# Joining two of three attention exponentials per group into one 1,024-column ScalarE instruction in a fused macaron transformer block

## The reference

```python
x = x + 0.5 * ffn(layernorm(x), W_up, W_gate, W_down)    # ternary weights, silu(up) * gate
x = x + attn(layernorm(x), Wq, bq, Wk, bk, Wv, bv)
x = x + 0.5 * ffn(layernorm(x), W_up, W_gate, W_down)
# attn: 16 query heads of 16 features, 4 key/value groups (4 query heads each), causal
scores = einsum('bhqd,bhkd->bhqk', q, k) / sqrt(d);  scores above the diagonal = -inf
out = einsum('bhqk,bhkd->bhqd', softmax(scores), v)
```

## Time and profile before

| | |
|---|---|
| median of three executions | 584.15 us |
| the profiled execution | 583.65 us |
| its span, first to last instruction | 581.9 us |
| TensorE busy | 554.8 us, 95% |
| VectorE busy | 480.2 us, 83% |
| ScalarE busy | 399.2 us, 69% |
| GpSimd busy | 168.5 us, 29% |
| 192 score matmuls (L1339) | first 206.9 us, last 409.2 us |
| 192 exponentials (L598), busy | 123.7 us |

### The profile page before, as it was taken

The page is one execution under the profiler, slowest core; times in us unless marked ns, Lnnn a source line. Parts: engine busy times, 40 slices in busy tenths (PEclk is TensorE's granted clock), DMA queues, the critical chain, the costliest instruction groups (busy, mean ns, idle before and its releaser), DMA issues.

```text
span 581.9 us, 12392 instructions
## 1 busy us (share of the span) xinstructions
PE 554.8 (95%) x4244; PEld 343.9 (59%) x4244; DVE 480.2 (83%) x1862; ACT 399.2 (69%) x716; POOL 168.5 (29%) x264
## 2 busy tenths in 40 slices
PE   2989999999999989999999999998999999999998
PEld 2445556656566756666566666554455656656566
DVE  6898978998875889999999998996897688666664
ACT  5857655765745469798888888887665765765642
POOL 3115201101440033555556463666301101110100
PEclk9999999999999999999999999999999999999999
DMA  8711101100104161323323323221302211111112
GB/s 304 235 30 37 19 19 37 37 20 19 38 0 116 34 148 58 90 73 85 102 52 103 85 67 85 69 50 39 38 1 58 52 55 55 37 56 55 36 37 73
DMA packets 72222, 37.90 MB, mean 65 GB/s; under 512 B 35520, under 2 KB 71616, under 8 KB 72128
## 3 DMA queue, kind: packets, MB, share of 16 engines
q1 hardware_dynamic: 72160, 37.11, 24.7%
HBM read 18.22 MB, written 10.49 MB: 49 GB/s over the span
## 4 chain that ended last, share of the span: by engine, by line
PE 77%; DVE 15%; ACT 3%; issue 2%; POOL 2%; DMA 1%; DVEq 0%; ACTq 0%; POOLq 0%
PE bank L1178 33%; PE bank L1190 17%; DVE sm_out L994 6%; PE bank L1339 5%; PE bank L1282 5%; PE bank L1309 5%; PE bank L1350 5%; PE bank L1364 2%; PE bank L1355 2%; PE bank L1154 1%; DVE hid L858 1%; DVE stats L738 1%; POOL xn L415 1%; ACT shared L598 1%; DVE hl L873 1%
## 5 line engine op out<-in xcount | busy, mean ns | idle before, releaser
L488 ACT ACTIVATE silu<-bank,w_scale 128x512 f32<-128x512 f32 x128 | 87.3, 683 | 114.1 <-PE bank L1178 114.1
L994 DVE CUSTOM_DVE_ANT_0 sm_out<-bank,mask 128x256 f16<-128x256 f32 (+1 forms) x512 | 151.0, 351 | 12.3 <-PE bank L1309 11.6
L858 DVE SCALAR_TENSOR_TENSOR hid<-silu,h_unit,bank 128x512 f32<-128x512 f32 x128 | 95.0, 743 | 63.5 <-ACT silu L488 63.1
L1190 PE MATMUL bank<-wT_down,hh 128*128 128x256 f16 x512 | 118.3, 273 | 2.5 <-DVE hl L873 2.3
L1190 PE MATMUL bank<-wT_down,hl 128*128 128x256 f16 x512 | 118.2, 272 | 0.0
L1178 PE MATMUL bank<-xh,wT_up 128*128 128x512 f16 x256 | 98.0, 383 | 1.1 <-DVE xl L802 0.7
L873 DVE TENSOR_TENSOR hl<-hid,hh 128x512 f16<-128x512 f32 x128 | 98.8, 772 | 0.0
L1178 PE MATMUL bank<-xh,wT_gate 128*128 128x512 f16 x256 | 97.3, 380 | 1.0 <-DVE hid L858 1.0
L1178 PE MATMUL bank<-xl,wT_up 128*128 128x512 f16 x256 | 98.0, 383 | 0.0
L1178 PE MATMUL bank<-xl,wT_gate 128*128 128x512 f16 x256 | 97.3, 380 | 0.0
L424 POOL TENSOR_TENSOR xnl<-xn,xnh 128x1024 f16<-128x1024 f32 x13 | 28.3, 2176 | 211.0 <-ACT xn L527 177.8
(11 more groups left out here) (134 smaller groups left out, 795.1 us busy)
## 6 DMA issues: line engine op xcount, KB each, us to landing
q_st<-q_scratch SPq DMA_DIRECT2D x32, 256.0 KB
q_scratch<-q_hl SPq DMA_DIRECT2D x16, 256.0 KB, 2.3
out_dram<-x SPq DMA_DIRECT2D x7, 512.0 KB, 3.0
x<-in_x_dram SPq DMA_DIRECT2D x1, 3072.0 KB, 15.5
k_scratch<-k_hl SPq DMA_DIRECT2D x16, 128.0 KB, 2.4
k_st<-k_scratch SPq DMA_DIRECT2D x16, 128.0 KB
x<-in_x_dram SPq DMA_DIRECT2D x2, 512.0 KB, 4.3
shared<-in_w_up_t_dram SPq DMA_DIRECT2D x2, 512.0 KB, 6.5
```

The source lines that it names most:

```text
L488: act.activation(silu[:, e % 2, :], U[e % 2][:, :], ACT.Silu, scale=w_scale[:, 0:1]).then_inc(silu_ready, 1)
L858: dve.scalar_tensor_tensor(out=hid[:, e % 4, :], in0=silu[:, e % 2, :], scalar=h_unit[:, 0:1], in1=GT[e % 2][:, :], op0=ALU.mult, op1=ALU. ...
L994: ins = dve.tensor_tensor_reduce(sm_out[:, i, cols], SM[i][:, cols], mask[:, S - size:S], -1.0 / MAX_UNIT, -MASKED, ALU.add, ALU.min, rowm ...
L1190: ins = pe.matmul(ACC[t % 2][:, 0:D], part[:, par, e, t * P:(t + 1) * P], wT_down[:, e, :], start=(e == 0 and part is hh), stop=(e == NE - ...
```

## The change

The two score banks are allocated as one tensor `twin` of 1,024 columns, with `bank[3]` and `bank[4]` as its halves. In groups 0 to 59, two of the three exponentials become one over both halves: parts 0 and 1 in even groups, parts 1 and 2 in odd groups. The joined instruction stands at the place of its later part, and adds 2 to `exp_done` when it has ended. The remaining part keeps its own instruction. All other code is as it was.

```diff
-        bank = [ctx.enter_context(nc.psum_tensor(f"bank{i}", [P, 512], F32)) for i in range(8)]
+        low = [ctx.enter_context(nc.psum_tensor(f"bank{i}", [P, 512], F32)) for i in range(3)]
+        twin = ctx.enter_context(nc.psum_tensor("twin", [P, 1024], F32))
+        high = [ctx.enter_context(nc.psum_tensor(f"bank{i}", [P, 512], F32)) for i in range(5, 8)]
+        bank = low + [twin[:, 0:512], twin[:, 512:1024]] + high
...
             def exps(n, parts):
                 for i in parts:
+                    twins = n < NG - G and i < 2 + n % 2 and i >= n % 2
+                    if twins and i == n % 2:
+                        continue
                     act.wait_ge(st_ready, 3 * n + i + 1)
-                    act.activation(PROB[n % 4][:, i, :], score_bank(n, i)[:, :], ACT.Exp,
-                                   scale=qk_scale[:, 4:5]).then_inc(exp_done, 1)
+                    if twins:
+                        act.activation(PROB[n % 4][:, i - 1:i + 1, :].rearrange("p i n -> p (i n)"), twin[:, :], ACT.Exp,
+                                       scale=qk_scale[:, 4:5]).then_inc(exp_done, 2)
+                    else:
+                        act.activation(PROB[n % 4][:, i, :], score_bank(n, i)[:, :], ACT.Exp,
+                                       scale=qk_scale[:, 4:5]).then_inc(exp_done, 1)
```

## The result

| | before | after |
|---|---|---|
| median | 584.19 us | 643.45 us |
| executions | 583.83 to 584.58 | 641.26 to 644.28 |
| profiled execution, span | 583.65, 581.9 | 641.26, 639.4 |
| the 60 joined sites, sum of the distances between the two score matmuls | 43.7 us | 103.1 us |

The ratio is 1.1009, 95% interval 1.0994 to 1.1024: 10% slower. Forecast were 624 us, between 611 and 645, and slower with 0.97. The sign, the place and the mechanism came out as forecast. The size did not: +59 us in place of +40.

A forecast was written before the change was run, and what follows sets the result against it. The prediction took TensorE's ordered list to bound the attention block. Its terms, 51 + 3 - 8.7 - 5.4 = +40 us on the profiled 583.65 us, gave 623.6, with the median 624 us, range 611 to 645.

The forecast's parts named there:

- The bound: Attention block: set by TensorE's ordered list, with small losses to VectorE and to exponentials.
- half hidden: Rival, attention block: VectorE nearly full too, absorbing more of TensorE's gaps; half of the 40 us, 604 us; chance 0.07.
- ScalarE's gain at nothing: Joined exponentials: ScalarE saves about 0.12 us a pair, 7 us in all, but has 25 us idle; costed at nothing.
- Required distance 1.57 us: Score matmuls around each pair: starts must lie 0.41 + 1.11 + 0.05 us apart, for landing, joined exponential and TensorE's release.
- the 51 + 3 of the prediction: Groups 0 to 59: +51 us of new stalls at the pair sites, +3 us for ScalarE's queue.
- ScalarE's queue, +3 us: Odd slots, twice a round: the queries' copy ends about 0.2 us after the later score lands; +3 us, between 0 and 8.
- What the stalls take over, -8.7 and -5.4 us: New stalls hide TensorE's row-maxima waits, -8.7 us, and the outputs' wait for the copied maxima, -5.4 us.
- GpSimd: Odd groups: causal selections start only after the joined exponential; outputs come later with 1 us to spare; nothing added.
- The clock: Rival: 1.2 GHz in a quarter of the attention block adds some 40 us, 665 us; chance 0.03.
- a slower exponential: Spread of the forecast: joined exponential of 1.056 to 1.23 us instead of 1.11, -3 to +7 us.
- a longer queue: Spread of the forecast: ScalarE's queue ahead of the joined exponential, -3 to +5 us.
- the outputs' term: Behind score part 2 of odd slots: the outputs' 5.4 us wait for copied maxima vanishes, -5.4 us.

The follow-up runs named there:

- the one with single exponentials in the new order: Kernel before, 192 single exponentials kept, with TensorE's outputs moved between parts 1 and 2 of even groups and the third max-score part behind part 2: 604.39 us.
- the one with lighter row maxima: Kernel before, with VectorE's row maxima of part 2 taken over 32 columns instead of 128 from group 4 on: 582.03 us, ratio 0.9967.
- The kernel with both start and release late: Changed kernel with two 512-column exponentials at the joined one's place, exp_done getting its 2 only at the second's end: 654.04 us, ratio 1.1188.

## Why the prediction was right or wrong

Point by point, by its own steps.

- **The bound.** Right: TensorE's ordered list. Every other engine's work went through unchanged in a block that was 57 us longer, and the rival "half hidden" is out.
- **ScalarE's gain at nothing.** Right, and the joined exponential takes 1.11 us, the value taken. The announced fall of ScalarE's busy time by 7 us did not come: the rows' lengths fell by 12.7 us, but their overlaps by 14.0 us. It has no effect on the sum.
- **Required distance 1.57 us.** The mechanism is right at every site; the size was 0.08 short at even sites and 0.17 at odd ones. Of this, 0.06 us is the later start of an exponential that adds 2 to its semaphore, and 0.08 us, at odd sites, is the score matmul's second wait; both were shown by taking them away. With both gone the growth is 54.0 us, which is the 51 + 3 of the prediction; that it fits so closely is in part luck, since the last of the 60 distances, 0.23 us before and after, did not grow at all: its wait comes one score matmul later, 0.6 us. Cost of the miss: 5.4 us.
- **ScalarE's queue, +3 us.** The two sites of a round with the queries' copy came out at 1.95 and 1.87 us in place of 1.65: 0.5 us a round, in the six rounds that have it, 3 us. Right.
- **What the stalls take over, -8.7 and -5.4 us.** This is the step that failed. Outside the sites, the distances between score matmuls of groups 0 to 59 together shrank by 4.2 us, not 14. (Those of the last four groups grew by 2.2 us: 0.6 us is the wait just named, 0.7 us one wait for GpSimd, and about 1 us a stretch at the lower clock; so all of them together shrank by 2.1 us.) The waits for row maxima did go, but I had added the weight loads' 6.1 us and the matmuls' 2.6 us, which are largely the same waits, and a weight load's idle time is not TensorE's. The matmuls' row alone, 2.6 us, would have been the better term. VectorE relieved by other means was worth 1.9 us. The 5.4 us of the outputs' weight loads were nothing at all: the outputs' first matmul starts 0.32 us behind the score in the changed kernel too, and its weight load still idles 0.23 us ahead of it, now without a releaser (the last two rows of the first timeline above). Cost of the miss: 10 us, and 2 us more in the last four groups.
- **GpSimd.** Right: from 232 to 457 us no wait of the outputs for a selection appears among the waits (there is one of 0.7 us, at 458.9), and odd pairs alone cost no more than their distances.
- **The clock.** Given 0.03 as a rival of +40 us; the profile of after was to show 1.00. It came, in small: some 1 to 4 us, below.

Sum by the measured terms: 59.4 us at the sites, -2.1 outside, makes 57.3; the span grew by 57.5 us. What is left to the medians' 59.3 is the clock, since the profiled execution was the quickest of the four. All the errors lie on one side. That 643 us is still within 611 to 645 is partly luck: the range left room for a slower exponential and a longer queue, which did not come, and none for the longer distances, for the outputs' term or for a little of the lower clock, which did.

By the figures of the Trainium skill, ScalarE: Activation LUTs, section What ACT_TABLE_LOAD costs, the estimate for the joined exponential was 1.13 us and for the saving 0.19 us a pair. The rows have 1.11 us, and the saving never reached the time.

## What to carry to other kernels

Where two buffers alternate between a producer that runs in order and a consumer, do not let one consumer instruction hold both: the fixed part that joining saves on the consumer (0.12 us here) is small against the overlap that it takes from the producer (1 us here). Read what a wait costs from the distances between starts of the engine's own instructions, in both places, and not from the sum of idle rows: weight loads and matmuls list the same wait twice. Before moving work into a stall, look at what that work was covering where it stood.

## What the runs showed of the hardware

**Adding 2 to a semaphore.** In the changed kernel ScalarE has 63 wait instructions of their own on the line ahead of the exponentials, where the kernel before has 3, though there are 60 exponentials fewer; the joined exponentials start 0.48 us behind their score in place of 0.42. Adding 1 brings back 3 and 0.42. The wait instructions on that line, in the changed kernel and then with the adding of 1:
```profile
L602 ACTq EVENT_SEMAPHORE  x63: 17/17/17, 207.7 to 465.7; - x63
```
```profile
L609 ACTq EVENT_SEMAPHORE  x3: 17/17/17, 454.8 to 463.9; - x3
```

**Two waits ahead of one matmul** cost 0.08 us of latency over one, here at the point where the engine stood and waited: 0.14 against 0.06 us.

**The granted clock fell for short stretches** in executions with many stalls; the kernel before, the one with even pairs alone, the one with single exponentials in the new order and the one with lighter row maxima had it at 1.00 in every execution. In the changed kernel, windows:
```profile
455.80:459.30 3.50, 1.98 (x13) 0.72 (x17) 1.76 (x2) 3.50 (x7) 2.69 (x4) 1.00 0.01 2
459.30:462.70 3.40, 3.08 (x34) 1.86 (x25) 0.69 (x1) 0.82 (x2) 1.27 (x4) 0.50 0.68 154
462.70:466.10 3.40, 3.40 (x38) 1.53 (x39) 1.95 (x5) 2.26 (x4) 1.39 (x3) 0.99 0.00 0
```
From 459.3 to 462.7 us TensorE was granted 0.50, the level of 1.2 GHz; before, it had been busy 1.98 of 3.5 us; afterwards it was back at 2.4 GHz. The kernel with both start and release late has six such stretches, the first of them:
```profile
210.70:214.10 3.40, 3.33 (x16) 2.23 (x15) 3.40 (x28) 0.75 (x2) 0.62 (x3) 0.50 0.56 144
```
They differ from execution to execution, and the times follow: the changed kernel took 641.26 us at a mean clock of 0.997, 642.66 at 0.995, 644.25 and 644.28 at 0.992; the kernel with odd pairs alone 613.78 at 0.997 and 612.54 to 612.59 at 1.00. As an estimate from these, with 0.997, 0.995 and 0.992 as one, two and three stretches, one costs 1.2 to 1.6 us. The Trainium skill, TensorE: Matmul & The Clock Gate, Part 1, has the clock fall after an idle stretch, and tells also of a kernel in which frequent short idles between groups of matmuls did it. The second is nearer to this case: TensorE idled no longer than 1.4 us ahead of any score matmul, and the granted clock fell all the same, with odd pairs alone in one execution of four; which of the stalls brought it on stays open.
